# Layer 0 of an interaction network from four product tiles instead of five, its squares made by ScalarE

## The reference

```python
for W in (W0, W1, W2):
    xk = relu(einsum('bmd,bhd,mhk->bkd', x0, xk, W))
    outs.append(sum(xk, axis=2))
h = concatenate([outs, dense_ctx], axis=1)
h = maximum(h @ W_top1 + b_top1, 0)
h = maximum(h @ W_top2 + b_top2, 0)
y = h @ W_top3
```

## Time and profile before

| | |
|---|---|
| median of 3 runs | 644.87 us (644.58 to 645.04) |
| the profiled execution | 644.13 us, span on the engines 642.3 us |
| TensorE clock granted | 1.00 of full speed throughout |
| DMA | 96.51 MB, mean 150 GB/s |
| PE, DVE busy | 584.2 us, 584.5 us |

### The profile page before, as it was taken

One profiled execution on the slowest core, in us unless ns is written; L12 is line 12 of the kernel. 1 busy time (PEld: TensorE's weight loads), 2 busy tenths in 40 slices (PEclk: granted clock), 3 DMA queues, 4 the chain that ended last, 5 costly groups with the idle time before them and its releaser, 6 DMA issues.

```text
span 642.3 us, 7779 instructions
## 1 busy us (share of the span) xinstructions
PE 584.2 (91%) x2896; PEld 209.1 (33%) x2896; DVE 584.5 (91%) x329; ACT 358.1 (56%) x594; POOL 469.8 (73%) x405
## 2 busy tenths in 40 slices
PE   0078999999998989999999999999999999999998
PEld 0023333232322323333334323333334323333455
DVE  1039899999999999999999999999999999999994
ACT  0006474657556465747676465747576565736552
POOL 6677769798888888888979788888979793803011
PEclk9999999999999999999999999999999999999999
DMA  5286596637181825547280826456370916300000
GB/s 162 46 320 155 220 289 166 264 65 298 35 284 50 259 106 153 212 80 285 53 310 5 278 85 195 170 119 245 64 300 15 299 53 202 160 3 2 1 2 1
DMA packets 27138, 96.51 MB, mean 150 GB/s; under 512 B 7414, under 2 KB 12540, under 8 KB 22876
## 3 DMA queue, kind: packets, MB, share of 16 engines
q1 hardware_dynamic: 18908, 93.90, 43.5%
q0 software_dynamic: 8192, 2.11, 2.7%
HBM read 80.25 MB, written 15.73 MB: 149 GB/s over the span
## 4 chain that ended last, share of the span: by engine, by line
DVE 42%; PE 27%; issue 12%; POOL 10%; DMA 5%; SPq 1%; ACT 1%; DVEq 0%; POOLq 0%; ACTq 0%
DVE prod L489 41%; PE acca L590 10%; PE accb L590 8%; POOL emb L362 7%; DMA rows<-field_dram 3%; PE acc L560 3%; POOL prod L380 3%; PE spread L633 2%; DMA field_dram<-zb_field 1%; PE accb L611 1%; PE acc L611 1%; SPq L280 1%; DVE prod L470 1%; DVE za L494 0%; ACT zb_field L720 0%
## 5 line engine op out<-in xcount | busy, mean ns | idle before, releaser
L362 POOL DMA_INDIRECT emb<-in_table,idx x256 | 247.2, 966 | 77.8 <-issue 67.6
L590 PE MATMUL acca<-prod,w 128*64 128x512 f32 x1024 | 229.1, 594 | 3.3 <-DVE prod L489 2.1
L590 PE MATMUL accb<-prod,w 128*64 128x512 f32 x960 | 216.4, 596 | 13.3 <-DVE prod L489 13.3
L380 POOL TENSOR_TENSOR prod<-rows,mates 128x1024 f32<-128x1024 f32 x70 | 164.4, 2380 | 16.0 <-issue 15.6
L489 DVE TENSOR_TENSOR prod<-rows,x1a 128x2048 f32<-128x2048 f32 x64 | 145.6, 2278 | 5.2 <-ACT x1a L725 2.5
L489 DVE TENSOR_TENSOR prod<-rows,x1b 128x2048 f32<-128x2048 f32 (+1 forms) x65 | 145.7, 2245 | 1.3 <-PE accb L590 0.7
L489 DVE TENSOR_TENSOR prod<-rows,x2a 128x2048 f32<-128x2048 f32 x64 | 145.7, 2277 | 1.1 <-PE accb L590 0.8
L489 DVE TENSOR_TENSOR prod<-rows,x2b 128x2048 f32<-128x2048 f32 x64 | 145.6, 2277 | 0.0
L590 PEld LDWEIGHTS acca<-prod,w 128*64 128x64 f32 x1024 | 71.7, 137 | 145.8 <-issue 136.1
L590 PEld LDWEIGHTS accb<-prod,w 128*64 128x64 f32 x960 | 65.6, 137 | 155.7 <-issue 113.7
L725 ACT ACTIVATE x1a<-acc 64x512 f32<-64x512 f32 x62 | 35.3, 570 | 124.5 <-PE acc L560 123.8
(11 more groups left out here) (74 smaller groups left out, 256.4 us busy)
## 6 DMA issues: line engine op xcount, KB each, us to landing
rows<-field_dram SPq DMA_DIRECT2D x30, 2048.0 KB, 13.6
field_dram<-zb_field SPq DMA_DIRECT2D x32, 256.0 KB
mates<-field_dram SPq DMA_DIRECT2D x16, 512.0 KB, 3.8
emb<-in_table,idx POOLq DMA_INDIRECT x256
field_dram<-zb_field SPq DMA_DIRECT2D x32, 128.0 KB
field_dram<-zb_field SPq DMA_DIRECT2D x16, 192.0 KB
rows<-field_dram SPq DMA_DIRECT2D x2, 1024.0 KB, 7.0
rows<-field_dram SPq DMA_DIRECT2D x1, 1536.0 KB, 12.6
```

Source lines behind the costliest of these rows:

```text
L362: pool.indirect_dma_start(out=emb[q % EMBS][:, j * EMB:(j + 1) * EMB], out_offset=None, in_=table, in_offset=bass.IndirectOffsetOnAxis(ap= ...
L380: nc.gpsimd.tensor_tensor(prod0[:, (q * L0 + k) % RING0, :], rows[:, slot(q, t), :], mates[:, :], ALU.mult).then_inc(s_prod0p, 1)
L590: mm = nc.tensor.matmul(acc[j % 2][side * HID:(side + 1) * HID, :], (w1 if layer == 1 else w2)[:, step, :], prod[:, (made(layer, s, half, ...
```

## The change

Layer 0 is computed from four product tiles and one tile of squares:

- `LAYER0_TILES` is now (1, 2, 3). A first product tile, `across` times `mates`, holds pairs of mixed distances: `across_of(q)` gives the field in each of its 128 rows. `across` is read from the list in four DMAs of 32 partitions.
- The squares of the 32 fields are made by ACT in a tile `squares` of 64 partitions (a half of the columns on 32 partitions each), read by two DMAs of 32 partitions (`fields_in`), squared in place by one instruction per period (`square_fields`), and summed by PE in two matmuls of 32 rows each, in place of a fifth tile's.
- `prod0` has four buffers for five. `h2`, an input of the tower, now lies in `h1`, to make room.
- In period 0 the row tiles come in the order 1, 2 and 3, 0, 4 to 7.

The sums over the 16 numbers are as they were. The core of the diff:

```diff
-LAYER0_TILES = (0, 1, 2, 3, 4)
-MATES = 104
+LAYER0_TILES = (1, 2, 3)
+MATES, FIELDS_LISTED = 104, 32
+def across_of(q):
+    return field_of(MATES + q % FIELDS_LISTED + 4 * (q // FIELDS_LISTED + 1))
...
-    FIRST = [(0, 2), (2, 2), (4, 1), (5, 3)]
+    FIRST = [(1, 1), (2, 2), (0, 1), (4, 4)]
...
-        SUM0[2 * q - 2, 1] = [(k, q) for k in range(3, L0)]
+        SUM0[2 * q - 2, 1] = [(SQUARES, q), (L0 - 1, q)]
...
+    ORDER0 = [*range(L0 - 1), SQUARES, L0 - 1]
...
                 sp.dma_start(mates[:, :], part).then_inc(s_mates, 16)
+                for b in range(BLOCKS):
+                    at = q % LISTS * LENGTH + MATES + 4 * (b + 1)
+                    part = bass.AP(field_dram.tensor, at * N, [[N, FIELDS], [1, N]])
+                    sp.dma_start(across[b * FIELDS:(b + 1) * FIELDS, :], part).then_inc(s_across, 16)
+            def fields_in(q):
+                wait_for(sp, s_l0, q * (L0 + 1))
+                for c in range(2):
+                    at = (q % LISTS * LENGTH + MATES) * N + c * HALF
+                    part = bass.AP(field_dram.tensor, at, [[N, FIELDS], [1, HALF]])
+                    sp.dma_start(squares[c * FIELDS:(c + 1) * FIELDS, :], part).then_inc(s_fields_in, 16)
...
                 mates_in(q)
+                fields_in(q)
                 for g in range(len(GROUPS)):
                     rows_in(q, g)
...
             def layer0(k, q):
+                if k == SQUARES:
+                    pe.wait_ge(s_squares, q + 1)
+                    for c in range(2):
+                        part = slice(c * FIELDS, (c + 1) * FIELDS)
+                        mm = nc.tensor.matmul(acc0[c * HID:(c + 1) * HID, :], w0[part, SQUARES, :], squares[part, :],
+                                              start=False, stop=False)
+                    mm.then_inc(s_l0, 1)
+                    return
...
+            def square_fields(q):
+                act.wait_ge(s_fields_in, (q + 1) * 2 * 16)
+                nc.scalar.activation(squares[:, :], squares[:, :], ACT.Square).then_inc(s_squares, 1)
             fields_out(0)
+            square_fields(0)
             input1(0, 0)
...
             input2(0, 1)
+            square_fields(1)
             input1(2, 0)
```

More of the change, by code:

```diff
@@ L186, in cin_tower_kernel @@
         mates = sb("mates", [P, N])
+        across = sb("across", [P, N])
+        squares = sb("squares", [2 * FIELDS, HALF])
         prod0 = sb("prod0", [P, RING0, N])
@@ L372, in product0 @@
             def product0(q, k):
-                t = LAYER0_TILES[k]
                 if k == 0:
                     pool.wait_ge(s_mates, (q + 1) * 16)
-                for g, (start, _) in enumerate(GROUPS):
-                    if t == start:
-                        pool.wait_ge(s_rows[g], q * 16)
-                wait_for(pool, s_l0, q * L0 + k - RING0 + 1)
-                nc.gpsimd.tensor_tensor(prod0[:, (q * L0 + k) % RING0, :], rows[:, slot(q, t), :], mates[:, :],
-                                        ALU.mult).then_inc(s_prod0p, 1)
+                    pool.wait_ge(s_across, (q + 1) * BLOCKS * 16)
+                if k == 1:
+                    pool.wait_ge(s_rows[0], q * 16)
+                wait_for(pool, s_l0, summed_before(q - 1, k) + 1)
+                other = across[:, :] if k == 0 else rows[:, slot(q, LAYER0_TILES[k - 1]), :]
+                nc.gpsimd.tensor_tensor(prod0[:, k, :], other, mates[:, :], ALU.mult).then_inc(s_prod0p, 1)
             def add_halves(z, n, done):
@@ L411, in _ @@
             gather_early(1)
-            pool.wait_ge(s_l0, L0)
+            pool.wait_ge(s_l0, L0 + 1)
             gather_early(2)
@@ L464, in product0 @@
             def product0(q, k):
-                t = LAYER0_TILES[k]
                 if k == 0:
                     dve.wait_ge(s_mates, (q + 1) * 16)
-                rows_wait(q, t)
-                wait_for(dve, s_l0, q * L0 + k - RING0 + 1)
-                nc.vector.tensor_tensor(prod0[:, (q * L0 + k) % RING0, :], rows[:, slot(q, t), :], mates[:, :],
-                                        ALU.mult).then_inc(s_prod0v, 1)
+                    dve.wait_ge(s_across, (q + 1) * BLOCKS * 16)
+                elif q == 0:
+                    rows_wait(q, LAYER0_TILES[k - 1])
+                elif k == 1:
+                    rows_wait(q, 0)
+                if q > 0:
+                    dve.wait_ge(s_l0, summed_before(q - 1, k) + 1)
+                other = across[:, :] if k == 0 else rows[:, slot(q, LAYER0_TILES[k - 1]), :]
+                nc.vector.tensor_tensor(prod0[:, k, :], other, mates[:, :], ALU.mult).then_inc(s_prod0v, 1)
             def outer(layer, s, half, u):
@@ L578, in layer0 @@
                     wait_for(pe, s_z1, q)
-                contract(acc0, w0[:, k, :], prod0[:, (q * L0 + k) % RING0, :], k == 0, k == L0 - 1).then_inc(s_l0, 1)
+                contract(acc0, w0[:, k, :], prod0[:, k, :], k == 0, k == L0 - 1).then_inc(s_l0, 1)
             def outer(j, half, u):
@@ L676, in _ @@
             pe.wait_ge(s_w0sum, 1)
-            for k in range(L0):
+            for k in ORDER0:
                 layer0(k, 0)
@@ L752, in input1 @@
                 if half == 0:
-                    act.wait_ge(s_l0, (s // 2 + 1) * L0)
+                    act.wait_ge(s_l0, (s // 2 + 1) * (L0 + 1))
                     relu_twice(x_of(1, s)[0], layer0_of(s), s_x1[0])
@@ L807, in tower_step @@
                     for j in range(TOP2 // P):
-                        done = nc.scalar.activation(h2[:, j, 0:width], tower[:, j * width:(j + 1) * width], ACT.Relu,
+                        done = nc.scalar.activation(h2_of(g)[:, j, :], tower[:, j * width:(j + 1) * width], ACT.Relu,
                                                     bias=b2[:, j:j + 1])
@@ L886 @@
     w0 = np.asarray(given.pop("L0_rec_W0"))
-    given["w0"], given["w0_swapped"] = np.zeros((2, 128, len(LAYER0_TILES), w0.shape[2]), w0.dtype)
+    given["w0"], given["w0_swapped"] = np.zeros((2, 128, len(LAYER0_TILES) + 2, w0.shape[2]), w0.dtype)
     seen = set()
-    for k, tile in enumerate(LAYER0_TILES):
+    for k in range(len(LAYER0_TILES) + 1):
         for q in range(128):
-            a, b = field_of(q + MATES), m[q, tile]
+            a, b = field_of(q + MATES), across_of(q) if k == 0 else m[q, LAYER0_TILES[k - 1]]
             if (a, b) not in seen:
@@ L896 @@
                 seen |= {(a, b), (b, a)}
+    for q in range(2 * FIELDS_LISTED):
+        a = field_of(MATES + q % FIELDS_LISTED)
+        assert (a, a) not in seen or q >= FIELDS_LISTED
+        given["w0"][q, len(LAYER0_TILES) + 1] = w0[a, a]
+        seen.add((a, a))
     assert len(seen) == w0.shape[0] * w0.shape[1]
```

24 lines of the change are left out of this document (17 added, 7 removed).

## The result

| | kernel before | changed kernel |
|---|---|---|
| median of 4 runs | 644.79 us (644.58 to 645.04) | 650.29 us (647.81 to 651.64) |
| ratio | | 1.008, 95% interval 1.0064 to 1.0096 |
| profiled execution | 644.13 us, span 642.3 | 647.81 us, span 645.7 |
| mean granted clock of TensorE | 1.000 | 0.997 in the profiled run, 0.995 in the others |

The kernel became slower by 5.5 us. The forecast was 646.1, its range 643.4 to 649.5: it missed. A second set of six runs gave 650.84 (647.03 to 653.11). The runs now spread over 4 to 6 us, where those of the kernel before lie within 0.5 (four runs) and 1.7 (nineteen). The profiled run is at the fast end; it lost 3.7 us, and the median lies 2.5 us above it.

The account below looks back on a forecast made before the run. It took DVE and PE as full (584.5 and 584.2 of 642.3 us), with transfers limiting the start. Terms 0.9 + 0.5 + 0.2 - 1.0 + 0.6 = +1.2 on the median 644.87 gave 646.1 us, range 643.4 to 649.5.

Parts of the forecast that it names:

- Term 1: Period 0: slow narrow reads delay tiles 2 and 3 to 44.9, so x1a begins at 49.2 for 48.30: +0.9 us.
- Term 2: Period 1: slot 1 on PE begins at 83.1 for 81.68, +1.4 in all, +0.5 us beyond period 0's delay.
- +3.3 for the reads of period 1: Period 1: `across` and `squares`, 0.66 MB ahead of the row tiles, delay them by up to 3.3 us; rows at 72.7.
- ACT's place of the squares: Period 1: ACT squares only behind x2b, now ending at 75.4; squared at 76.0, and this, not the transfer, sets the time.
- Terms 3 and 5: PE-led places: +0.2 us in layer 0 of period 2; +0.6 us at two tower steps and the end.
- d: Extra PE time of the squares' pair from changing tile shape there and back: 0.2 us, bounds 0 and 0.4.
- slack: Steady part: a period has 0.29 us before DVE feels PE being late, so the squares cost nothing there.
- Term 4: Steady part: PE's waits for POOL in periods 3 and 4 go, as POOL drops 14 products: -1.0 us.
- The serial pair: Rival: the squares' two matmuls run one after the other, costing 1.06 us extra per pair: +15, 660 us; chance 0.07.
- A dearer change of shape: Rival: PE's change of tile shape costs more than 0.1 each, 0.4 us per squares' pair: +3.6, 648.5 us; chance 0.15.
- The saving arrives: Rival: DVE's two fewer products ahead of 75 us save 2.4 us and POOL's stalls go: -3.4, 641.5 us; chance 0.10.
- full-rate transfers: Rival: reads into 32 partitions run at 400 GB/s: -0.1 to -1.1, middle 644.3 us; chance 0.18.

Follow-up runs that it names:

- e0: The changed kernel run again without edits, as yardstick of a later batch: 650.84 us, ratio 1.0093 to the kernel before.
- e3: Changed kernel with the last row piece of period 0 held back until the gather of period 1 has landed: 648.83 us, ratio 1.0074.
- e4: Changed kernel with four more filler matmuls on PE in period 0, two in each of two waits: 650.69 us, ratio 1.0083.
- e14: Changed kernel with six more filler matmuls, four in PE's two waits of period 0 and two in period 1: 648.97 us, ratio 1.0069.
- e1: Changed kernel without the reads into `squares`; ACT squares the first 32 partitions of `mates` in two activations: 648.79 us, ratio 1.0073.
- e6: Changed kernel with squares from `mates`, the last row piece of period 0 behind the gather, and four filler matmuls: 647.88 us, ratio 1.0061.
- e12: Changed kernel with squares made from `mates` in an already summed product slot, summed as an ordinary 128-row pair: 647.18 us, ratio 1.0038.
- e2: Changed kernel with `across` read from 128 consecutive list rows in one two-level transfer; layer 0 not the reference's: 648.36 us, ratio 1.0052.
- e15: Changed kernel with `across` from 128 consecutive list rows in one three-level transfer; layer 0 not the reference's: 648.48 us, ratio 1.0059.
- e13: Changed kernel with periods 0 and 1 as before; from period 2 squares written into the product slot as an ordinary pair: 643.20 us, ratio 0.9974.
- e7: Changed kernel with `across` by one three-level read of 128 partitions, same addresses, blocks four rows apart: 678.37 us, ratio 1.0390.
- e8: Changed kernel with `across` by one three-level read, blocks four rows apart, and squares from `mates` without own reads: 675.42 us, ratio 1.0320.
- e9: Changed kernel with `across` by one three-level read, squares from `mates`, last row piece behind the gather, four filler matmuls: 679.64 us, ratio 1.0393.
- e16: Repeat on another chip of the changed kernel with `across` by one three-level read, blocks four rows apart: 675.23 us (one run).

## Why the prediction was wrong

**Term 1 failed**, "period 0, +0.9". The step that failed is the landing of tiles 2 and 3. The sum let half a megabyte of narrow reads delay it by 1.3 us, to 44.9; it came 2.6 us late, at 46.20. From there to x1a it went nearly as forecast (4.42 us for 4.3). So x1a came at +2.3, and the copy of the fields, on which period 1 hangs, at +2.6.
- *The rate of narrow reads was right, their cost was not.* The forecast charged 1.3 us for `across` and nothing for `squares`, whose reads are issued behind tiles 2 and 3. From the issue of `mates` to the product of tile 2 the kernel before takes 8.99 us (34.63 to 43.62); with `across` and `squares` read narrow it is 11.77, 11.47, 11.10, 12.77 and 11.36 in five profiles (the changed kernel, e0, e3, e4, e14; mean 11.7), without the reads of `squares` 10.43, 11.15 and 11.28 (e1, e6, e12; mean 11.0), with `across` wide 10.67 and 9.41 (e2, e15; mean 10.0). By the means `across` costs 2.0 for 1.3 and `squares` 0.7 for nothing. The 0.7 is rough, since the two sets of values touch, but the rate shows its source: in all seven profiles that read `squares` there is a slice of 1 us between 43 and 46 with 223 to 260 GB/s at a full share (in the changed kernel 244 at 44, in the window above 268), while tiles 2 and 3 are due, and in e1, e6 and e12 every slice at a full share there has 348 or more.
- *The gather* was no term; in the changed kernel it adds 0.3 to the copy. PE got it at 52.53, when the DMA share had gone from 0.85 (50 to 51) to 0.14 (52 to 53); in e3, where the last row piece waits for the gather, it was in by 49.3. And it would have eaten most of what faster reads gain (e15).
- *The clock*, foreseen nowhere. It is not in the profiled run's loss: there it fell only over the filler, and slot 1 waited for rows. In e0's profile (649.13 us) it fell to 0.50 near 48.6, ahead of the last sums, and the windows show it:

```profile
48.00:50.00 2.00, 2.00 (x8) 0.37 (x8) 0.34 (x1) 0.00 (x0) 0.00 (x0) 0.66 1.01 408
50.00:52.00 2.00, 1.80 (x4) 0.12 (x4) 0.00 (x0) 0.15 (x1) 0.00 (x0) 0.50 0.60 242
52.00:54.00 2.00, 1.67 (x17) 1.17 (x18) 0.87 (x1) 1.95 (x4) 1.61 (x2) 0.50 0.04 4
```

The squares' pair and the next took 1.63 and 1.98 us for 1.07 and 1.08, and slot 1 began at 86.32, 1.2 later than in the profiled run. Variants that keep the narrow reads (e3, e4, e6, e14) take 647.3 to 648.8 in their nine runs at a clock of 1.000; the changed kernel's ten runs take 647.0 to 647.8 at 0.997, 649.1 to 651.8 at 0.992 to 0.995, and 652.5 and 653.1 at 0.987 and 0.990. So of its 5.5 us some 3 are there at a full clock. The 2 to 3 beyond come in runs in which the clock fell, and four traces (e0, e2, e3, e4) show it stretching sums on the path; in e0 this puts slot 1 1.2 us later. That it makes all of them is not shown: no run of the changed kernel above 650 has a trace, and in the only such trace of these variants, e4's, the transfers made more of the excess than the clock.

**Term 2** was near in size, 0.8 (3.46 less the copy's 2.6) for 0.5, but not in its path. Slot 1 missed the forecast by 2.0 us, of which 1.7 are term 1's. The +3.3 for the reads of period 1 was 3.5 (61.95 to 74.60 is 12.65 us, before 9.17). The forecast let ACT's place of the squares set the time; in the trace ACT squares at 76.97 and is done at 77.6, while PE sums products until 78.03: the rows that landed at 74.60 set it. The reason for the 3.5 is only partly shown: with wide reads (e2, e15) it still needs 12.4, without those of `squares` 12.2 to 12.6. The half megabyte at 400 GB/s is 1.3 of these 3.2; the rest stays open.

**Terms 3 and 5** were right in mechanism, wrong in size: d is 0.3 and not 0.2. Slot 2's place was +0.29 (3.75 at 117.80 against 3.46 at slot 1) for 0.2, the tower steps and the end +1.0 for 0.6 (2.72 by 188.74 to 3.73 at 618.61). d is just what the forecast had read as slack, 0.29 us, and no steady period stalls: DVE is 2.72 us late at 188.74 and 2.77 at 362.10. The forecast's 0.1 per change came from one between 64 and 128 columns; to 32 rows and back costs 0.3 for both.

**Term 4** was right: DVE's lateness falls from 3.75 to 2.72, -1.03 for -1.0; e13 keeps it, 363.76 against 364.57 in spite of +0.24 at its start.

The sum of the profiled run: 3.46 + 0.29 - 1.03 + 1.0 = +3.7 for +1.2. Of the 2.5 that were missed, 1.7 are term 1's, 0.3 term 2's, 0.1 term 3's and 0.4 term 5's.

**The rivals.** The serial pair is refuted: 1.00 us from start to start (218.45 to 219.45), for 0.86 of an ordinary pair and 1.92 (0.86 + 1.06) by this rival. The pair's two matmuls write the two 64-partition halves of `acc0`, and their four records, 0.61 us each by the median, take 1.07 us together: they overlap, as those of an ordinary pair do (eight records of 0.59 us in 1.89 us at 215.63). A dearer change of shape (d = 0.4, 648.5 us) came nearest in time, by luck: d is 0.3, and most of the loss lies elsewhere. "The saving arrives" and "full-rate transfers" fell with the 210 GB/s: against the 400 of the wide reads the earlier trace rows it is 0.53, where the list's 197 is 0.49.

## What to carry to other kernels

At a place that waits for transfers, count every read in flight, those issued behind the awaited one too, and ask what else (here a gather) lands only when the traffic drains (52.53 us, for 49.3 at the latest in e3). Price a wait by the engine that the chain goes through: PE's 1.96 us for the gather were worth 0.3 us, because ACT was busy for most of them. Ask as well what stands idle meanwhile: in or behind waits of 1.8 to 3.1 us TensorE's granted clock fell to 0.50 in eight of the traces here (the changed kernel, e0 to e4, e12, e15), at times just when its work arrived. That cost and the transfers' own vary from run to run, so one profile can understate the loss. A change that pays in the steady part may be kept out of the start: the same four products from period 2 on, with the squares as an ordinary 128-row pair, turned +0.8% into -0.26% (e13).

## What had not been expected of the hardware

- One DMA of 0.52 MB in three levels with blocks four rows apart delayed DVE's first product to 47.9 to 50.3 us in four profiles on two chips (e7, e8, e9, e16), where four DMAs of the same bytes gave 41.1 to 42.8 in nine profiles and one of 128 plain rows 40.1 and 39.8. In e16 it completed in four landings, where the reads of `across` and of the row tiles in e2 and e15 have 16 each. All reads beside it were slow too: 217 and 204 GB/s at shares of 0.98 and 1.02 (e16, 42 to 46).
- Two reads of 64 KB into 32 partitions, issued behind tiles 2 and 3, brought the rate down to 223 to 260 GB/s for a slice of 1 us while these tiles were due, in each of seven profiles.
- The granted clock fell to 0.50 in or behind waits of 1.8 us (e12) to 3.1 us (e15) of a PE that was otherwise busy, not in the same place in every run and not behind each of them (e14's profiled run waits 2.1 us at a full clock). With two waits of period 0 filled, it fell in period 1 (e4, 0.50 near 78.6, behind a wait of 2.75 us). The waits of up to 1.6 us that the kernel before has after 40 us left it at 1.00.
- At the start the profile's clock row says 1.00 in both kernels, but the matmuls do not run like it: the same 16 transposing records take 1.09 us at 25.23 and 0.68 at 49.57, the same ten filler records 6.06 us at 34.76, behind a wait of 8.4, and 4.56 at 50.18 (kernel before). Nothing waited for the filler at 34.76.
- Chips differ: the kernel before took 653.0 us on one of them (median of 13 runs, clock 0.995 to 0.997) and 644.6 to 644.8 on the others (clock 1.000). Its cause was not looked into.
